# A typed-attention pass with broadcast destination rows, three-part look-ups and precomputed run ends; weights loaded beside a loop

## The reference, cut to what matters

```python
q_dst = Q[dst]
k_src = K[src]
for et in range(N_ETYPES):
    m = (edge_type == et)[:, None, None]
    kt = jnp.where(m, jnp.einsum('ehd,hdf->ehf', k_src, W_edge[et]), kt)
scores = (q_dst * kt).sum(-1) / jnp.sqrt(jnp.float32(HD))
scores = scores * mu[:, edge_type].T
smax = jax.ops.segment_max(scores, dst, num_segments=N)
ex = jnp.exp(scores - smax[dst])
den = jax.ops.segment_sum(ex, dst, num_segments=N)
w = ex / (den[dst] + 1e-10)
agg = jax.ops.segment_sum(V[src] * w[..., None], dst, num_segments=N)
```

## Time and profile before

| what | value |
|---|---|
| median of 3 runs | 5562.72 us |
| profiled execution | 5571.87 us (span 5570.1 us) |
| PE busy | 3508.8 us, 63% |
| POOL busy | 2989.3 us, 54% |
| DVE busy | 2833.7 us, 51% |
| ACT busy | 775.1 us, 14% |
| trA, first gather to the end of the last | 637.7 us |

### The profile page before, as it was taken

How to read it: one execution, slowest core, us unless ns; L and a number is a source line. 1 busy time by engine, 2 the same in 40 slices (tenths; PEclk the granted TensorE clock), 3 DMA queues, 4 the chain that set the end, 5 groups by cost and what they waited for, 6 DMA issues and landing times. The chain is left out here.

```text
span 5570.1 us, 81908 instructions
## 1 busy us (share of the span) xinstructions
PE 3508.8 (63%) x19282; PEld 3012.5 (54%) x19283; DVE 2833.7 (51%) x8668; ACT 775.1 (14%) x1756; POOL 2989.3 (54%) x2911
## 2 busy tenths in 40 slices
PE   0000599867777577847645444568887999556665
PEld 0000488856666466735624433357676898246663
DVE  5100388854444344444796443357666555344443
ACT  1000022221111111112100000211111000312222
POOL 3777577736777377720035776058887000047772
PEclk9999998975555555557555555765555555789998
DMA  5233455533223122224502333244444333012222
GB/s 206 73 77 79 111 156 150 149 64 86 76 75 72 53 76 76 77 33 135 120 15 61 78 79 62 70 140 128 125 126 119 98 112 85 6 53 62 63 62 34
DMA packets 538364, 490.42 MB, mean 88 GB/s; under 512 B 229590, under 2 KB 443800, under 8 KB 538264
## 3 DMA queue, kind: packets, MB, share of 16 engines
q0 software_dynamic: 99328, 211.51, 16.0%
q1 hardware_dynamic: 369048, 202.79, 13.1%
q10 hardware_dynamic: 69888, 75.00, 5.1%
HBM read 366.59 MB, written 122.43 MB: 88 GB/s over the span
## 5 line engine op out<-in xcount | busy, mean ns | idle before, releaser
L625 POOL DMA_INDIRECT ring<-table_gine,idx x1248 | 1243.4, 996 | 574.6 <-issue 363.7
L1569 PE MATMUL ps<-msg,oh 128*128 128x128 f32 (+1 forms) x3328 | 680.0, 369 | 280.8 <-DVE HA L671 275.9
L625 POOL DMA_INDIRECT ring<-table_msg,idx x416 | 421.9, 1014 | 756.6 <-SPq L187 630.1
L1569 PEld LDWEIGHTS ps<-msg,oh 128*128 128x128 f32 x3328 | 592.0, 267 | 358.4 <-DVE HA L671 306.2
L655 POOL DMA_INDIRECT arena<-table_keys_values,idx x416 | 511.3, 1229 | 331.5 <-SPq L187 205.1
L671 DVE TENSOR_TENSOR mraw<-ps,ring 128x512 f32<-128x512 f32 x416 | 287.0, 690 | 789.1 <-DMA ring<-table_gine,idx 506.7
L1578 PE MATMUL ps<-wt,ear 64*128 64x128 f32 x2496 | 568.7, 396 | 43.0 <-DMA ear<-edge_attr_T 43.0
L671 DVE TENSOR_TENSOR HA<-HA,ps 128x128 f32 (+1 forms) x1664 | 475.8, 286 | 170.3 <-DVE HA L671 150.4
L1578 PEld LDWEIGHTS ps<-wt,ear 64*128 64x128 f32 x2496 | 486.4, 288 | 104.4 <-issue 92.7
L611 POOL DMA_INDIRECT slot_records<-arena,slotr x400 | 393.4, 983 | 200.4 <-issue 121.2
L671 DVE TENSOR_TENSOR oh<-iota_n,dl 128x512 f32<-128x512 f32 x624 | 429.1, 688 | 48.0 <-DVE small L671 27.6
(11 more groups left out here) (297 smaller groups left out, 6429.5 us busy)
## 6 DMA issues: line engine op xcount, KB each, us to landing
ear<-edge_attr_T SPq DMA_DIRECT2D x312, 128.0 KB
oh<-slot_rows ACTq DMA_DIRECT2D x104, 256.0 KB, 4.5
ear<-slot_rows ACTq DMA_DIRECT2D x208, 128.0 KB, 2.9
slot_values<-arena SPq DMA_DIRECT2D x104, 256.0 KB, 3.3
ring<-slot_values SPq DMA_DIRECT2D x104, 256.0 KB, 3.1
slot_records<-msg SPq DMA_DIRECT2D x32, 650.0 KB, 11.1
arena<-slot_records SPq DMA_DIRECT2D x104, 200.0 KB
edge_attr_T<-arena ACTq DMA_DIRECT2D x104, 192.0 KB
```

The costliest lines, as they stand in the source:

```text
L625: pool.indirect_dma_start(out=ring[:, k % 4, j, 0:width], out_offset=None, in_=table[:, :], in_offset=bass.IndirectOffsetOnAxis(ap=idx[:, ...
L1569: ins = M.matmul(out_of(t, j), oh[:, t.s4, j, :], x, start=True, stop=True)
```

## The change

It rebuilds the first pass and moves some loads.

- The transposed one-hot no longer comes from DVE, PE and ACT. ACT starts a DMA per batch that broadcasts the batch's destination row to 128 partitions (`drow`), and DVE compares it in bf16 with the partition number (`oT`). Q is held as three bf16 parts (`QB`), so the look-up is 12 bf16 matmuls per batch and exact.
- The run ends of equal destinations and the scan's resets depend on the graph alone. They are worked out once in `slot_rows` of GINE round 1: the resets go to DRAM (`reset_rows`, four DMAs of 104 x 8 rows) and SP brings 32 rows of 512 B per batch back (`rz`); the ends are folded into `dl_end`, which makes the second one-hot select only end slots. The scan reads the scores straight from PSUM.
- The weights of Q, V and K (24 of the 32 pieces) are loaded beside the relational attention; their clearing moves there too. Q is split on DVE in `tr_qv`.

```diff
+        resets = dram("reset_rows", [NT, NHEAD, P])
...
+                    sp.wait_ge(dve_made, ends_set)
+                    for g in range(NG4):
+                        sp.dma_start(resets[g * GT:(g + 1) * GT], RSD[:, g, :].unsqueeze(1).to_broadcast([GT, NHEAD, P])).then_inc(rowsd_out, 16)
...
-            join.to("tr_clear")
-
+            sp.wait_ge(dve_made, gm_set)
             for h in range(NHEAD):
...
+            join.to("tr_clear")
+            for h in range(NHEAD):
+                s = slice(h * HD, (h + 1) * HD)
                 load(WEb[s, :, s], a["L2_gnn_W_edge"][:, h].rearrange("t d f -> d t f"))
...
+            def resets_of(k):
+                if k >= 4:
+                    sp.wait_ge(qm["scanned"], k - 3)
+                sp.dma_start(rz[:, k % 4], resets[k * B:(k + 1) * B].rearrange("t h s -> (t h) s")).then_inc(resets_in[k % 4], 16)
+            for k in range(4):
+                resets_of(k)
             for k in range(NB):
+                if k >= 8:
+                    resets_of(k - 4)
                 sp.wait_ge(qm.gath[k % 4], 16 * B * (k // 4 + 1))
                 sp.wait_ge(values_out[k % 4], 16 * (k // 4))
                 sp.dma_start(vals[k].rearrange("p (j d) -> p j d", j=B), kvring[:, k % 4, :, D:2 * D]).then_inc(values_out[k % 4], 16)
+            for k in range(NB - 4, NB):
+                resets_of(k)
             join.to("tr_zero")
...
+                ch(V.memset(NED, 1.0))
+                ch(tt(NED[:, :, 1:P], row16[:, 1, :, 1:P], row16[:, 1, :, 0:P - 1], ALU.not_equal))
+                ch(V.tensor_scalar(RSD, NED[:, :, 0:P], -4 * BIG, None, ALU.mult))
...
+                ch(V.tensor_scalar(dl_end[:, :], dl[:, :], 1.0, None, ALU.add))
+                dve.wait_ge(pe_made, ends_turned)
+                ch(tt(dl_end[:, :], dl_end[:, :], ps[:, 4, 0:NT], ALU.mult))
+                ch(V.tensor_scalar(dl_end[:, :], dl_end[:, :], -1.0, None, ALU.add))
...
+            ch(V.memset(wt[:, 0:WK_o + NTYPE * D], 0.0))
...
+            def scan_max(t):
+
+                dve.wait_ge(qm["rows"], t.n + 1)
+                dve.wait_ge(resets_in[t.s4], t.u * 16 + 16)
+                if t.late(2):
+                    dve.wait_ge(qm["back"], t.n - 1)
+                V.tensor_tensor_scan(sf[:, t.h, :], rz[:, t.s4, :], ps[0:B * NHEAD, 4 + t.h, 0:P], 0.0, ALU.add, ALU.max).then_inc(qm["scanned"], 1)
+
+            def end_onehots(t):
+                if t.late(4):
+                    dve.wait_ge(qm["sums"], t.n - 3)
+                tt(oh[:, t.s4], iota_n[:, :].unsqueeze(1).to_broadcast([P, B, P]),
+                   dl_end[:, bass.ds(t.k * B, B)].unsqueeze(2).to_broadcast([P, B, P]), ALU.is_equal).then_inc(qm["onehot"], 1)
+
+            def max_dst_onehots(t):
+                t2 = Batch(t.r, t.s, 1)
+                dve.wait_ge(drin[t.s4], t2.u * 16 + 16)
+                if t.late(2):
+                    dve.wait_ge(qm["node"], t.n - 1)
+                V.tensor_scalar(oT[:, t.h, 0], drow[:, t.s4], iota_p, None, ALU.is_equal).then_inc(qm["onehotT"], 1)
...
-                    got = ps[:, 7, t.h * 64:t.h * 64 + B * w].rearrange("p (j c) -> p j c", j=B)
+                    got = ps[:, 6 + t.h, 0:B * w].rearrange("p (j c) -> p j c", j=B)
...
-            ch(V.memset(wt[:, 0:WK_o + NTYPE * D], 0.0))
             ch(V.memset(WE, 0.0))
+            ch(V.memset(gm[:, :, :, NHEAD:NHEAD + 1], 1.0))
...
+            join.to("tr_keysT")
+            for b0 in range(0, NBLK, 5):
+                dve.wait_ge(pn_free, QV_EVACS + b0 + 5)
+                split([v[:, b0:b0 + 5, :] for v in QB], Qn[:, b0:b0 + 5, :], q_rest)
...
-                ch_tr.step(V.tensor_scalar(small3[:, t.s4, 32:64].rearrange("p (j g) -> p j g", j=B),
-                                      dl[:, bass.ds(t.k * B, B)].unsqueeze(2).to_broadcast([P, B, NHEAD]), 0.0, None, ALU.add))
-                yield
-                ch_tr.done()
...
-            run(dve, [(11, acc_max(NHEAD)), (4, tr_score), (7, scan_max(NHEAD)), (7, onehots(qm["onehot"], qm["sums"], oh)),
-                      (0, onehots(onehot_tr, qm["turned"], ohx, lambda t: t.k))])
+            run(dve, [(9, acc_max(NHEAD)), (3, tr_score), (5, scan_max), (6, end_onehots), (1, max_dst_onehots)])
...
-                A.activation(gm[:, t.s4, :, 0:NHEAD], ps[:, 6, o:o + B * NHEAD].rearrange("p (j g) -> p j g", j=B), ACT.Copy)
-                A.activation(gm[:, t.s4, :, NHEAD:NHEAD + 1], ps[:, 6, o + 32:o + 32 + B * NHEAD].rearrange("p (j g) -> p j g", j=B)[:, :, 0:1],
-                             ACT.Copy).then_inc(qm["picked"], 1)
...
-            run(act, [(6, score_rows(NHEAD)), (9, picked), (2, onehotT(qm, lambda t: t.k))])
+                A.activation(gm[:, t.s4, :, 0:NHEAD], ps[:, t.h, 0:B * NHEAD].rearrange("p (j g) -> p j g", j=B), ACT.Copy).then_inc(qm["picked"], 1)
+
+            def max_rows_in(t):
+                if t.late(4):
+                    act.wait_ge(qm["onehotT"], t.n - 3)
+                act.dma_start(drow[:, t.s4], slotrow[1:2, bass.ds(t.k * B, B), :].rearrange("w t s -> w (t s)")
+                              .to_broadcast([P, B * P])).then_inc(drin[t.s4], 16)
+            run(act, [(7, picked), (0, max_rows_in)])
...
+            def turn_scores(t):
+                pe.wait_ge(qm["scores"], t.n + 1)
+                if t.late(2):
+                    pe.wait_ge(qm["scanned"], t.n - 1)
+                M.transpose(ps[0:B * NHEAD, 4 + t.h, 0:P], small3[:, t.s4, 0:B * NHEAD], ident[:, :]).then_inc(qm["rows"], 1)
+
+            def turn_maxima(t):
+                pe.wait_ge(qm["scanned"], t.n + 1)
+                if t.late(2):
+                    pe.wait_ge(qm["picked"], t.n - 1)
+                pe.sem_inc(pe_go, 1)
+                M.transpose(ps[:, t.h, 0:B * NHEAD], sf[:, t.h, :], ident[0:B * NHEAD, 0:B * NHEAD]).then_inc(qm["back"], 1)
+
+            def max_lookups(t):
+                pe.wait_ge(qm["onehotT"], t.n + 1)
+                if t.late(2):
+                    pe.wait_ge(qm["scores"], t.n - 1)
+                blocks = blocks_of(pe, PE, t)
+                for j in range(B):
+                    for i in range(3):
+                        ins = M.matmul(ps[:, 2 + t.h, j * P:(j + 1) * P], oT[:, t.h, 0, j * P:(j + 1) * P],
+                                       QB[i][:, bass.ds(blocks[j], 1), :].rearrange("p a d -> p (a d)"), start=(i == 0), stop=(i == 2))
+                ins.then_inc(qm["node"], 1)
+
+            def max_sums(t):
+                pe.wait_ge(qm["onehot"], t.n + 1)
+                pe.wait_ge(qm["picked"], t.n + 1)
+                if t.late(2):
+                    pe.wait_ge(qm["ch_acc"], t.n * 2 - 2)
+                for j in range(B):
+                    ins = M.matmul(ps[:, 6 + t.h, 9 * j:9 * j + 9], oh[:, t.s4, j, :], gm[:, t.s4, j, 0:9], start=True, stop=True)
+                ins.then_inc(qm["sums"], 1)
...
-            run(pe, [(10, sums(qm, 0, lambda t, j: ps[:, 7, t.h * 64 + 9 * j:t.h * 64 + 9 * j + 9], ready="picked", taken="ch_acc",
-                              rhs=lambda t, j: gm[:, t.s4, j, 0:9])),
-                     (3, node_rows(qm, rows_at(Qn, D), lambda t, j: ps[:, 2 + t.h, j * P:(j + 1) * P], local, "scores")),
-                     (5, turn_scores(NHEAD)), (8, turn_maxima(NHEAD)), (1, turn_onehot(qm, local, None, ohx))])
+            run(pe, [(8, max_sums), (2, max_lookups), (4, turn_scores), (6, turn_maxima)])
```

More of the change, by code:

```diff
@@ L151, in build @@
         bn_done = sem("feature_statistics")
-        onehot_tr = sem("onehot_for_turning")
+        resets_in = [sem(f"reset_rows_in{h}") for h in range(4)]
         relv_ps = sem("rel_vectors_in_psum")
@@ L304, in build @@
         qg = Sems("gine", "edge", "onehot", "added", "relu", "sums", "acc", gath=True, ea=True)
-        qm = Sems("max", "onehot", "turned", "onehotT", "node", "scores", "rows", "rows_sb", "scanned",
+        qm = Sems("max", "onehot", "onehotT", "node", "scores", "rows", "scanned",
                   "back", "picked", "sums", "acc", "ch_scan", "ch_acc", gath=True)
@@ L384, in build @@
         muv = small[:, 0, 0:NHEAD * NREL]
-        ohx = T[0][:, 0:2 * B * P].rearrange("p (h b d) -> p h b d", h=2, b=B)
+        flat_ring, flat_msg = (v[:, :, :, :].rearrange("p a b d -> p (a b d)") for v in (ring, msg))
+        QB = [v[:, 0:NPAD // 2].bitcast(BF16).rearrange("p (b d) -> p b d", b=NBLK) for v in (flat_ring, flat_msg, AG)]
+        q_rest = mraw[:, :, :, :].rearrange("p a b d -> p (a b d)")[:, 0:5 * D].rearrange("p (b d) -> p b d", b=5)
+        NED = T[2][0:GT, 0:NG4 * (P + 1)].rearrange("p (g s) -> p g s", g=NG4)
+        RSD = T[2][0:GT, 1024:1024 + NG4 * P].rearrange("p (g s) -> p g s", g=NG4)
         kwb = T[0][:, 0:2 * NREL * D].rearrange("p (h r d) -> p h r d", h=2, r=NREL)
@@ L1414, in onehotT @@
                 return body
-            def score_rows(n):
-                def body(t):
-                    act.wait_ge(qm["rows"], t.n + 1)
-                    if t.late(2):
```

(4 more changed lines are left out.)

65 lines of the change are left out of this document (11 added, 54 removed).

## The result

The changed kernel, called after below, takes 5486.7 us (median of 4 runs, 5484.0 to 5492.7), the kernel before 5560.2 beside it: a ratio of 0.986, with a 95% interval of 0.984 to 0.989, or 73.5 us less. The forecast was 5465, the range 5432 to 5520. The profiled executions lie 85.2 us apart (spans 5570.1 and 5484.9), so the terms of the sum are compared with that.

A forecast was written before the change was run, and what follows sets the result against it. POOL was taken as the first pass's bound, its gathers stretched by VectorE's two-SBUF-input instructions. Terms -89.0 - 3 - 11.2 + 3.4 + 2 = -97.8 us, against the median 5562.7, gave 5465 us; range 5432 to 5520.

The forecast's parts named there:

- What bounds the loop: First pass: POOL bounds at 5.00 us a batch; DVE tensor_tensors with two SBUF inputs stretch gathers, 1.14 us a batch.
- first pass, period: First attention pass: 5.28 us a batch, -89.0 us; forecast case 5.1 to 5.45 (5446 to 5483 us), 45%.
- tail of it: First pass, last gather to first split of the maxima: 9 turns instead of 11, plus a reset landing, -3 us.
- weights: 24 of 32 weight loads, 0.465 us each, move beside the relational loop where SP has no other work: -11.2 us.
- splitting Q: Splitting Q on DVE: the last group follows ACT's last copy and delays the join, +3.4 us (bounds +2, +4).
- head of the second GINE loop: Second GINE loop's start: more DVE operations and four reset DMAs delay the first sum, costing 0 to 6 us: +2.
- `oT` by itself looks harmless: First pass: the bf16 compare alone stretches no gather, since the relational loop's 153 gathers with it average 946 ns.
- The new wait: First pass: the scan's wait for its reset row stays hidden from POOL with 1.6 us to spare; nothing added.
- a sign that the forecast had named for being wrong: First pass: POOL idle before its gathers would show the forecast wrong; DVE's scan should wait for resets, POOL never for scores.
- the ring: Rival, first pass: reset landings bound the loop from 5.4 us; at 11.1 the period is 7.17, 5661 us in all; 4%.
- Parked one-hots: Rival, first pass: one-hots still hold a gather in every batch, period 5.75, -40.2 us, 5514 in all; 20%.
- a free POOL: Rival, first pass: the one-hot falls between gathers' early moments, period 5.00, -118.0 us, 5436 in all; 25%.

The follow-up runs named there:

- E4: The changed kernel with a second, unread f32 one-hot ahead of the end one-hot in each batch of the first attention pass: 5553.8 us in one run.
- E2: The changed kernel with the one-hots of first pass, second and third GINE loop and message loop by four tensor_scalars each: 5422.9 us, ratio 0.9737.
- E6: The kernel before with only the weights' loads and the clearing of their tile moved as in the change: 6150.3 us, ratio 0.9977.
- E1: The changed kernel with the first attention pass's f32 end one-hot by four tensor_scalars instead of one tensor_tensor: 5494.9 us, ratio 0.9865.
- E5: The changed kernel with SyncE issuing the scan's resets two batches earlier, on the second chip: 6173.1 us, ratio 1.0012 to the kernel before.
- E10: The same edit as E5 (the changed kernel, resets two batches earlier), on the third chip: 6166.6 us, ratio 1.0016 to the kernel before.
- E3: The kernel before with only both f32 one-hots of the first attention pass by four tensor_scalars each: 5513.6 us, ratio 0.9897.

## Why the prediction was right, and where it was off

**What bounds the loop** was read rightly. E4 put work on VectorE that it had room for, and the period grew by 0.45 us; E2 took away the two SBUF inputs, and two loops fell to 5.00 and a third to 5.05. The inference of the Trainium skill that was doubted (SBUF — State Buffer, "Who interferes with whom": a tensor_tensor doesn't hold up descriptor generation) is contradicted by E2 and by 109 of 114 moments in the first pass.

| term | forecast | measured |
|---|---|---|
| first pass, period | -89.0 (5.28 us) | -81.7 (5.35) |
| tail of it | -3 | +3.7 |
| weights | -11.2 | -10.2 to -11.9 (E6) |
| splitting Q | +3.4 | +2.4 to +4.1, -7.8 with the weights |
| head of the second GINE loop | +2 | 0.0 in this pair of profiles, not resolved |
| sum | -97.8 | -85.8 |

**The time** missed by 21.8 us (5486.7 against 5464.9). 12.6 are the sum's. The rest is that the sum, worked out from one profile, was taken off the median: the kernel before was profiled in an execution 11.7 us above its median, the changed one in an execution at its median, so the profiles differ by 85.2 and the medians by 73.5. The period came inside the forecast's 5.1 to 5.45, the time 4 us outside its 5446 to 5483; it is the range that held.

**The period** was taken from the nearest loops with one f32 one-hot, and 0.07 us were missing, 7.3 us in all. The weak step is "`oT` by itself looks harmless": it stands behind `oh` without a gap, and the row ends with it, 0.3 us later; 47 of 51 long gathers end 0.8 us behind `oT` and not behind `oh`. But no run takes `oT` out of the row, and 0.07 us is no more than executions differ by: the second GINE loop, with the same code, ran at 5.17 us a batch in the changed kernel, at 5.24 in E1 and at 5.25 in E4. That 5.28 came so near is in part luck.

**The new wait** was reckoned with 1.6 us to spare for POOL, at a landing of 3.3 us; the scans that waited started 3.7 us behind the issue, and POOL waited twice, 5.2 us in all. By its letter that is a sign that the forecast had named for being wrong, though 5.2 us of 555 change nothing. What the step didn't see is how near the ring is: as soon as E1 makes gathers shorter, POOL waits 23 times.

**The tail** has the wrong sign, and the forecast had named the reason and not followed it to the end of the loop. It said that SyncE issues the resets of batch b behind the landing of b+3. For the last four batches that wait is the last landing, with nothing beside it any more, and that landing is late in either kernel: the last values leave 8.6 us (changed) and 10.0 us (before) behind the start of the last gather. The two turns that were saved are eaten by it, and 8 us come back when two of the four go earlier (E5, E10).

**The weights and Q** came as reckoned. **The head of the GINE loop** was reckoned rightly in its parts. The four resets' issues hold SyncE from 1271.47 for 6.30 us, and POOL stalls 4.3 us for the first sum, inside the 0 to 6 of the forecast:

```profile
1271.47 6.30 SPq L490 DMA_DIRECT2D reset_rows<-arena  x4
...
1277.82 10.12 SPq L483 DMA_DIRECT2D ear<-edge_attr_T  x4
...
1286.79 1.15 POOL L646 DMA_INDIRECT ring<-table_gine,idx  x1 [4.56 <-DVE mraw L692]
```

In this profile it is made up for in the loop, where the fourth gathers average 1.04 us instead of 1.11. That is no effect of the stall: E1 and E4 have the same stall (4.5 and 4.2 us) and averages of 1.11 and 1.13. The 0.0 of the table is a coincidence of two executions.

**The rivals.** Parked one-hots (5.75) and a free POOL (5.00) both didn't come; the loop drifts between them, with a long gather in every second batch instead of in each. The ring isn't the bound at a landing of 3.7 us. What the two other chips showed was no rival at all: that another resource than POOL can be the bound for the same kernel, and then the sign of the change turns.

## What to carry to other kernels

In these kernels a gather issued by GpSimd pays for the longer instructions of VectorE with two SBUF inputs that run just after its start, and what follows one without a gap can prolong the hold. Look for gathers that end a fixed time behind such a row (0.8 us here), and make the one-hot with tensor_scalars and a column of scalars (here 72 us, nearly all in three loops). When a load is put behind a wait for "three batches later", follow its last issues past the end of the loop. Extra bytes can be expected to be free only where transfers are not the bound, and what the bound is differed from chip to chip here: measure a change that trades engine time for bytes on more than one.

## What the runs showed of the hardware that I had not expected

- Two chips on which the kernel before takes 6160 us instead of 5560. `mraw` starts there 15.8 us behind the last gather of its batch instead of 1.8 (third GINE loop), the gather loops other than the first pass take 5.8 to 6.9 us a batch (E6) instead of 5.0 to 5.35 (before, on the first chip), and a megabyte takes as much time of the DMA engines as elsewhere. All 56 runs of before on them lie between 6142 and 6186 us.
- Four tensor_scalars of 128x128 f32, 0.84 to 1.00 us, let a gather start and end beside them in 0.94 us, where one tensor_tensor of 128x512, 0.68, held it to 1.4.
- Tensor_scalars are not always harmless: in the first pass 28 of 56 gathers (E1) that met them were lengthened, by 0.1 to 0.8 us, and behind the mask of E3 they kept 39 gathers held.
- A pause of 0.03 to 0.04 us between two tensor_tensors let a gather through; without one it was held to the end of the second.
